# Walsh-Hadamard prologue of a two-layer transformer kernel: the two upper butterfly levels over row blocks moved from VectorE and GpSimd to TensorE

## The reference, cut to what matters

```python
def fwht(x):                      # along the last axis, n = 2048
    h = 1
    while h < n:
        xb = x.reshape(-1, n // (2 * h), 2, h)
        a, b = xb[:, :, 0, :], xb[:, :, 1, :]
        x = jnp.stack([a + b, a - b], axis=2).reshape(-1, n)
        h *= 2
    return x / np.sqrt(n)

hidden = jax.nn.silu(up_gate) * up_lin
hidden = fwht(hidden)
out = jnp.einsum('bsh,dh->bsd', hidden, W2)
```

## Time and profile before

| | us |
|---|---|
| median of 3 runs | 3669.11 (3665.75 to 3682.47) |
| profiled execution, its own time | 3674.73 |
| its span, first to last instruction | 3672.8 |
| TensorE busy over the span | 3160.3 (86%) |
| end of this stage, first instruction of the next | 70.39 |

### The profile page before, as it was taken

The page is one execution under the profiler, slowest core; times in us unless marked ns, Lnnn a source line. Parts: engine busy times, 40 slices in busy tenths (PEclk is TensorE's granted clock), DMA queues, the critical chain, the costliest instruction groups (busy, mean ns, idle before and its releaser), DMA issues. The chain is left out here.

```text
span 3672.8 us, 46449 instructions
## 1 busy us (share of the span) xinstructions
PE 3160.3 (86%) x16049; PEld 2444.9 (67%) x16049; DVE 1891.4 (51%) x3951; ACT 1250.5 (34%) x2773; POOL 1576.3 (43%) x1491
## 2 busy tenths in 40 slices
PE   2999999899999899999989999995988873087886
PEld 0778777687787777777778777774766662044443
DVE  6455555645555555555564555554644565811110
ACT  2444444334333434344333343343322311022221
POOL 3366666535455534454552545452132131033333
PEclk9999999999999999999999999996998886599998
DMA  5533232422212242122232221114022112199886
GB/s 163 171 118 107 84 118 102 151 99 78 83 58 75 95 152 87 58 75 87 84 119 103 75 87 58 65 36 147 30 80 92 49 46 70 33 270 246 246 247 172
DMA packets 208555, 396.33 MB, mean 108 GB/s; under 512 B 21072, under 2 KB 95696, under 8 KB 207696
## 3 DMA queue, kind: packets, MB, share of 16 engines
q1 hardware_dynamic: 194000, 357.87, 29.2%
q0 software_dynamic: 14336, 35.66, 4.6%
HBM read 290.08 MB, written 103.32 MB: 107 GB/s over the span
## 5 line engine op out<-in xcount | busy, mean ns | idle before, releaser
L749 POOL TENSOR_SCALAR probs<-probs,comb 128x512 f32<-128x512 f32 (+3 forms) x384 | 221.6, 586 | 1042.2 <-DVE comb L706 1042.0
L861 ACT ACTIVATE probs<-score_ps,neg_max 128x640 f32<-128x640 f32 (+7 forms) x512 | 374.4, 738 | 482.0 <-DVE neg_max L712 482.0
L712 DVE TENSOR_REDUCE neg_max<-score_ps 128x2 f32<-128x256 f32 (+7 forms) x256 | 347.4, 1357 | 116.2 <-PE score_ps L983 115.6
L754 POOL TENSOR_TENSOR probs<-probs 128x512 f32<-128x512 f32 (+3 forms) x384 | 384.2, 1015 | 10.7
L758 POOL TENSOR_TENSOR out_root<-out_root,neg_half 128x16 f32<-128x16 f32 x128 | 372.6, 2912 | 6.6 <-DVE out_root L689 6.6
L784 ACT ACTIVATE attT<-turn_ps 128x512 fp32r<-128x512 f32 (+3 forms) x384 | 189.1, 492 | 472.0 <-PE turn_ps L892 469.1
L614 DVE TENSOR_TENSOR layer_sum<-product_ps,layer_sum 128x512 f32<-128x512 f32 x384 | 263.2, 685 | 38.3 <-PE product_ps L61 32.6
L980 PE MATMUL score_ps<-keys_all,queries_all 64*128 64x512 f32 (+3 forms) x2304 | 276.8, 363 | 0.0
L601 DVE TENSOR_TENSOR attT<-turn_ps,attT 128x512 fp32r<-128x512 f32 (+3 forms) x384 | 213.0, 555 | 109.7 <-ACT attT L784 107.1
L659 DVE SCALAR_TENSOR_TENSOR hidden<-gate_tanh,product_ps 128x512 f32<-128x512 f32 x128 | 88.1, 688 | 298.4 <-ACT gate_tanh L826 298.4
L980 PEld LDWEIGHTS score_ps<-keys_all,queries_all 64*128 64x128 f32 x2304 | 186.6, 185 | 67.2 <-issue 30.7
(11 more groups left out here) (252 smaller groups left out, 7279.9 us busy)
## 6 DMA issues: line engine op xcount, KB each, us to landing
w_qk<-weights_split SPq DMA_DIRECT2D x48, 512.0 KB, 4.5
w_gate<-weights_split SPq DMA_DIRECT2D x48, 512.0 KB, 3.2
w_up<-weights_split SPq DMA_DIRECT2D x48, 512.0 KB, 3.6
w_down<-weights_split SPq DMA_DIRECT2D x48, 512.0 KB, 6.2
e_gate_up<-in_w_gate_dram SPq DMA_DIRECT2D x64, 384.0 KB, 4.0
e_gate_up<-in_w_up_dram SPq DMA_DIRECT2D x64, 384.0 KB, 5.4
e_down<-in_w_down_dram SPq DMA_DIRECT2D x64, 384.0 KB, 6.6
values_by_head<-hidden_split SPq DMA_DIRECT2D x32, 512.0 KB, 3.3
```

Source lines behind the costliest of these rows:

```text
L712: dve.tensor_reduce(nmax[:, i % 2, :], score_tile(i % NT), AX.X, ALU.max, negate=True)\
L749: pool.tensor_scalar(PR[:, r, 1, c], PR[:, r, 1, c], comb[:, i % 4:i % 4 + 1], 1.0, ALU.mult, ALU.mult)\
L754: pool.tensor_tensor(PR[:, r, 0, c], PR[:, r, 0, c], PR[:, r, 1, c], ALU.add).then_inc(s_comb, 1)
L861: act.activation(PR[:, i % 2, q, 0:(j + 1) * P], score_tile(j)[:, q, :], ACT.Exp, bias=nmax[:, i % 2, q:q + 1], accum_out=sums[:, i % 16, ...
```

## The change

Only `hadamard_w2` is changed. `LEVELS` becomes 2: the butterflies that pair neighbouring blocks and blocks two apart stay on VectorE and GpSimd, inside a chunk of four row blocks. The two upper levels combine whole chunks. They are now part of the product: output chunk k of a piece is the sum over the piece's four chunks g of H hi(g) + H lo(g), with the matrix or its negative (`had_minus`, made once by ScalarE) according to the parity of k & g. So an output chunk takes 8 matmuls in place of 2, and needs `hi` and `lo` of all four chunks of its piece. `hi` and `lo` get 8 buffers each (two pieces). VectorE does two `low` after each level in place of one; ScalarE's order becomes `hi` of piece q's chunk k, then `scaled` of piece q-1's chunk k, in turn, and its `hi` of piece q first waits for the products of piece q-2.

```diff
--- before.py
+++ after.py
@@ -73,7 +73,7 @@
     ND = D // PIECES
     CB = 4
     NB = NC // CB
-    LEVELS = int(math.log2(NC))
+    LEVELS = int(math.log2(CB))
     with ExitStack() as ctx:
         def sb(name, shape, dt=F32):
             return ctx.enter_context(nc.sbuf_tensor(name, shape, dt))
@@ -84,8 +84,9 @@
         bufs = [sb("had_ping", [P, PIECES, NC, ND]), sb("had_pong", [P, PIECES, NC, ND])]
         h_f = sb("had_f", [P, P])
         h_r = sb("had_r", [P, P], F32R)
-        hi = sb("had_hi", [P, 2, CB * ND], F32R)
-        lo = sb("had_lo", [P, 2, CB * ND], F32R)
+        h_n = sb("had_minus", [P, P], F32R)
+        hi = sb("had_hi", [P, 2 * NB, CB * ND], F32R)
+        lo = sb("had_lo", [P, 2 * NB, CB * ND], F32R)
         out = sb("had_out", [P, 4, CB * ND])
         ps = ctx.enter_context(nc.psum_tensor("had_ps", [P, 2, CB * ND], F32))
         s_in, s_c, s_h = [sem(f"had_in{i}") for i in range(PIECES)], sem("had_const"), sem("had_hr")
@@ -134,9 +135,9 @@
             @block.vector
             def _(dve):
                 def low(i):
+                    n = i % (2 * NB)
                     dve.wait_ge(s_hi, i + 1)
-                    dve.tensor_tensor(lo[:, i % 2, :], chunk(i), hi[:, i % 2, :].bitcast(F32), ALU.subtract)\
-                       .then_inc(s_lo, 1)
+                    dve.tensor_tensor(lo[:, n, :], chunk(i), hi[:, n, :].bitcast(F32), ALU.subtract).then_inc(s_lo, 1)
 
                 for q in range(PIECES):
                     dve.wait_ge(s_in[q], 16)
@@ -151,7 +152,8 @@
                         dve.tensor_tensor(split(b[:, :, 1])[0], split(a[:, :, 0])[0], split(a[:, :, 1])[0], ALU.subtract)\
                            .then_inc(s_dif, 1)
                         if q:
-                            low((q - 1) * NB + level)
+                            for k in range(NB // LEVELS):
+                                low((q - 1) * NB + level * (NB // LEVELS) + k)
                 for k in range(NB):
                     low((PIECES - 1) * NB + k)
 
@@ -173,6 +175,7 @@
             def _(act):
                 act.wait_ge(s_c, 16)
                 act.activation(h_r[:, :], h_f[:, :], ACT.Copy).then_inc(s_h, 1)
+                act.activation(h_n[:, :], h_f[:, :], ACT.Copy, scale=-1.0).then_inc(s_h, 1)
 
                 def scaled(i):
                     act.wait_ge(s_mm, i + 1)
@@ -181,27 +184,34 @@
                     act.activation(out[:, i % 4, :], ps[:, i % 2, :], ACT.Copy, scale=0.5 / math.sqrt(HID))\
                        .then_inc(s_out, 1)
 
-                for i in range(PIECES * NB):
-                    if i >= 2:
-                        scaled(i - 2)
-                    if i % NB == 0:
-                        n = (i // NB + 1) * LEVELS
-                        act.wait_ge(s_sum, n)
-                        act.wait_ge(s_dif, n)
-                        act.wait_ge(s_dif2, n)
-                    act.activation(hi[:, i % 2, :], chunk(i), ACT.Copy).then_inc(s_hi, 1)
-                scaled(PIECES * NB - 2)
-                scaled(PIECES * NB - 1)
+                for q in range(PIECES + 1):
+                    for k in range(NB):
+                        i = q * NB + k
+                        if q < PIECES:
+                            if k == 0:
+                                act.wait_ge(s_sum, (q + 1) * LEVELS)
+                                act.wait_ge(s_dif, (q + 1) * LEVELS)
+                                act.wait_ge(s_dif2, (q + 1) * LEVELS)
+                            if q >= 2:
+                                act.wait_ge(s_mm, (q - 1) * NB)
+                            act.activation(hi[:, i % (2 * NB), :], chunk(i), ACT.Copy).then_inc(s_hi, 1)
+                        if q:
+                            scaled(i - NB)
 
             @block.tensor
             def _(pe):
-                pe.wait_ge(s_h, 1)
+                pe.wait_ge(s_h, 2)
                 for i in range(PIECES * NB):
-                    pe.wait_ge(s_lo, i + 1)
+                    q, k = divmod(i, NB)
                     if i >= 2:
                         pe.wait_ge(s_out, i - 1)
-                    pe.matmul(ps[:, i % 2, :], h_r[:, :], hi[:, i % 2, :], start=True, stop=False)
-                    pe.matmul(ps[:, i % 2, :], h_r[:, :], lo[:, i % 2, :], start=False, stop=True).then_inc(s_mm, 1)
+                    for g in range(NB):
+                        pe.wait_ge(s_lo, q * NB + g + 1)
+                        h = h_n if bin(k & g).count("1") % 2 else h_r
+                        n = (q * NB + g) % (2 * NB)
+                        pe.matmul(ps[:, i % 2, :], h[:, :], hi[:, n, :], start=(g == 0), stop=False)
+                        ins = pe.matmul(ps[:, i % 2, :], h[:, :], lo[:, n, :], start=False, stop=(g == NB - 1))
+                    ins.then_inc(s_mm, 1)
 
 
 def layer0(nc, x, wqk, wvT, woT, lam, w1T, w3T, w2p, ident_d, mask_d, v_d, split_d, x2, batches):
```

## The result

The first comparison, 20 runs of each kernel: 3666.35 us (median; 3654.64 to 3680.62) against 3677.82 for the kernel before (3665.75 to 3686.38), ratio 0.9972 with a 95% interval of 0.9960 to 0.9984. So the change makes the kernel faster, by less than 0.5%: 10.2 us by the means, with a standard error of 2.0. Forecast was a gain of 16.4 us. Five executions of either kernel, in the later sets, took over 450 us longer than the rest; they are left out of every number here. The profiled execution took 3659.19 us, its span is 3657.4, and the stage that was changed ends at 55.15 us where it ended at 70.39: 15.2 us earlier.

What follows compares the result with a forecast made beforehand. VectorE bounds the stage before, TensorE after: from 19.95 us, 5.1 + 25.4 = 30.5 ends its stream at 50.45, the stage at 54.0, 16.4 us gained. 3669.1 - 16.4 gives 3653 us, range 3645 to 3667.

Steps and rivals of the forecast that it cites:

- TensorE's unbroken run: In the changed stage, TensorE works through 124 matmuls without a gap of weight from 19.95 us, 30.5 us long.
- twelve products at the low level: At the start of TensorE's stream, 12 matmuls (between 8 and 16) take 0.428 us each, the other 112 take 0.2265.
- the tail of 3.8 us: After TensorE's stream: last output 0.2 us, scaling 0.60, store issue 0.02, and 2.76 to the next stage.
- the start of the run: TensorE waits for low(2) behind piece 1's next level, then starts its 124 matmuls at 19.95 us.
- 3.42 + 0.60 = 4.02: Butterfly levels with two lows: 3.42 us from level to level with one low, 0.60 more on VectorE for the second.
- after 18 us no DMA runs: Reading of the stage before the change, used to say that the loads are no obstacle; piece 1 lands at 10.2 us.
- The clock's swing: Small gaps between pieces or chunks return TensorE to the low clock level repeatedly; price 10 us, gain 6; chance 0.10.
- The clock that never rises: TensorE's 124 matmuls all at 0.428 us, 53.1 us; next stage at 76.5, 6 us slower; chance 0.05.
- the longer interval in each pair: Each group's wait stops the next weight load running ahead, 0.31 us instead of 0.23; +5.3 us, gain 11; chance 0.10.
- VectorE or ScalarE as the bound: A costlier second low or late hi makes lows slip 2 to 3 us, TensorE stalls about 2; gain 14; chance 0.10.
- The 131 ns per matmul: Skill-page price for 512-column matmuls, weighed but not used: VectorE and ScalarE would end the stage near 48 us, gain 22.
- taken off the median, 3669.1 - 16.4 = 3652.7: Whole-kernel time: the stage's 16.4 us gain subtracted from the median of the runs shown, giving 3653 us.

Runs made afterwards that it cites:

- hi_only: The changed kernel without the products of lo (64 matmuls for 128); read from one profile, the stage ends at 48.66 us.
- the four sets: Changed kernel, unedited, timed against the kernel before in four comparisons: 10.2, 12.3, 14.9 and 16.4 us below by the means.
- kept_busy: The changed kernel plus 110 unused 128-column matmuls before TensorE's first products and in its first pause; stage ends at 65.70 us, ratio 0.9986 to the kernel before.
- busy_wide: The changed kernel plus 28 unused 512-column matmuls ahead of and between TensorE's first products; stage ends at 53.79 us, ratio 0.9950 to the kernel before.

## Why the prediction was right or wrong

**The stage.** The mechanism was right in the main: levels of 3.0, then (behind the first with lows) 4.0 to 4.3 us; TensorE's unbroken run; twelve products at the low level, in fact ten and a part of the eleventh; 0.2276 us for the others where 0.2265 was taken; the tail of 3.8 us. VectorE's lows were never late for it: the last needed one, low(15), ends at 44.5 (started at 43.85), and chunk 12 wants its last group at about 45.7 (51.57 - 4 x 1.82 + 1.36). In each of the pieces 1 to 3 the last low is ready 1.1 us ahead, where the prediction had 0.5 to 1. Forecast 54.0, profile 55.15. The miss of 1.15 us is the start of the run, 21.18 for 19.95; the rest of the sum came out within 0.1 us. The first load came 0.25 us later than in the profile before, and the first level with two lows took 5.09 us where "3.42 + 0.60 = 4.02" stood. In this level a GpSimd operation runs beside the sum (2.29 us) and another beside the second low (1.76 us); in the later ones beside the sum alone, beside the second low alone (1.1 and 1.3 us), or beside neither. That term was mis-sized by 1.07 us, once; the later levels take 4.02 to 4.27. One reading beside it was too wide: "after 18 us no DMA runs" holds for the loads; the first store is issued at 23.8 us before and at 23.9 after.

**The rivals.** The clock's swing (first) did not come: in the changed kernel TensorE does not pause from 21.18 on. `hi_only`, where it pauses, shows it. The clock that never rises (second) did not come. Nor did the longer interval in each pair (third): it would have shown as 0.31. VectorE or ScalarE as the bound (fourth) is refuted by the full 25 us of TensorE and by `hi_only`; what the fourth rival said of a second low that costs more than 0.60 us did come, once, and only moved the start. The 131 ns per matmul of the Trainium skill (page "TensorE: Matmul & The Clock Gate", section "Back-to-back issue gap") did not come either: the trace has 0.2276 us.

**The time.** Here the step that failed is the baseline: "taken off the median, 3669.1 - 16.4 = 3652.7". Three runs gave 3669.1; twenty, these three among them, gave 3677.8, and the profiled run, 3674.7, lay between. Against the twenty the forecast of 3653 is a drop of 24.8 us, more than twice the 11.5 by which the medians differ. With 20 runs as the base the same sum gives 3661.4; measured were 3666.35. The 13.4 us between forecast and median are thus 8.7 of baseline, 1.2 of the stage, and 3.5 that the stage does not explain: spread of the runs, or time given back behind it. That 3666.35 still lies inside the range of 3645 to 3667, by 0.65 us, is luck: the upper side was made for rivals 1, 3 and 4, and none of them came. The spread I had put at a few microseconds for a median, but one of three runs from a spread of 5.6 to 7.2 us (standard deviation of single runs in the first comparison) has one of about 4 alone, and this one was off by twice that.

**The chances.** 0.64 stood for no more than 0.5% and 0.33 for more. All sets together give 13.6 us, 0.37%, so the larger chance was on the right side. Wrong was the reason given beside it, that 0.5% is about what a measurement can tell from no change: with 20 runs of each the interval of 0.9960 to 0.9984 tells 0.3% from none.

**What stays open.** 13.6 us (0.85) against 15.5 in the profiles is a gap of about two standard errors, and the four sets differ among themselves (10.2 to 16.4) by a little more than their own errors allow. A give-back of 1 to 3 us behind the stage is neither shown nor excluded; in the profiles the rest is 3602 to 3624 us after (mean 3610.7 of six) and 3602 to 3613 before (3608.2 of three), far too wide to see it. The stretch up to the token table alone, without the scattered writes, has 2464.0 us after and 2462.9 before in the mean, but the six after spread with a standard deviation of 3.0.

## What to carry to other kernels

When work moves to another engine, work out when that engine can start without a gap, not only how much it gets: here the end of the stage is the start of TensorE's run plus 124 matmuls, and it followed that start almost one to one. When two engines share turns, each operation added in front of a turn may let the other engine in, so price it from a row in which both have something waiting: here a second low cost 1.67 us (5.09 for 3.42) and not 0.60. And before a change of 0.4% is forecast in absolute time, look at how far the few runs of before can lie from their own mean.

## What the runs showed of the hardware

- Matmuls of 128 columns in fp32r, one behind the other at the low level, cost 0.214 us each in `kept_busy`, nearly as much as 512 columns at the high level (0.2276); behind 17.1 us of them the clock was still low, as the interval of 0.43 us shows. In `busy_wide` it rose at 10.9 us, during the seventh of a row of matmuls of 512 columns that began at 7.99.
- The granted clock reads 1.00 for stretches in which the matmuls are at the low level: in this stage before (pairs 0.60 us apart that last 0.63) and in `kept_busy` from 24 to 32 us (the products from 24.72 to 26.00 are 0.43 apart). The trace has no record of the clock before its first rise, at 96.6 us in the one and 35.8 in the other. Up to there the interval between starts is the measure, not that column.
- From the first to the last of the 64 scattered writes it is 440.7 us in one profile of the changed kernel and 451.9 in another: 11 us of difference, more than half of the stage's saving.
